# Attention passes: partial sums of a group handed to VectorE in two parts, by PSUM bank

## The chip, the cores and the metric

One core of one Trainium2 chip runs the whole program. The metric is the device time of one launch in microseconds (us). The kernel before takes 9238.56 us (median of 3 runs, 9234.02 to 9243.33).

## The reference, cut to what matters

Four graph layers over 6250 nodes and 106,250 edges (50,000 both ways and one loop per node), the edges sorted by destination. The two layers that the change touches are attention layers:

```python
# L1: 4 heads of 32
x_l = x @ W_l + b_l;  x_r = x @ W_r + b_r
e = einsum(leaky_relu(x_l[src] + x_r[dst]), att)            # a score per edge and head
alpha = softmax of e over the edges of one dst
out = segment_sum(alpha * x_l[src], dst)
# L2: 1 head of 128
h = x @ W;  e = leaky_relu((h @ att_src)[src] + (h @ att_dst)[dst])
alpha = softmax of e over the edges of one dst
out = segment_sum(alpha * h[src], dst)
```

Each is added to the nodes and normalised, then comes the next layer. All in float32.

## The kernel before, in words

The function `attend` runs twice: `attend1` for L1 (`two_sided`, table `xl_table`, rows of 136 values) and `attend2` for L2 (`h_table`, rows of 129 values). Between the two, and after the second, other stages run; a stage begins when the one before it has ended on all engines.

The edges lie in tiles of 128. A **group** is G = 7 tiles; there are R = 126 groups; a **chunk** is CG = 9 groups. Since the edges are sorted by destination, those of one tile fall on a window of at most 128 neighbouring nodes that begins at `base`. The result `acc` holds features on the partitions and nodes along the free axis, so that a tile's contribution is added to `acc[:, base : base + 128]`.

A step of the pass is one turn of the loop over g (142 of them, `last_step = R + LAG + 1`), with LAG = 15 and a ring of RING = 19 gathered groups:

- **GpSimd** (POOL) issues 7 indirect DMAs per group, the gathers of `rows` (L1494). It waits only for a free slot of the ring (`msg_ready`).
- **SyncE** (SP) loads one-hot rows, node windows and flags.
- **TensorE** (PE) does, in this order in step g: `expand(g)` (L1554, L1557: what the destination gives, into `ps_x`), transposes of the softmax of a chunk in the steps that have one, `sums(g - 15)` (L1566: for each of 7 tiles one float32 matmul of messages and one-hot matrix, two passes each, into `ps_sum`), `fill_d(g - 14)` (L1537, into `ps_d`), more transposes.
- **ScalarE** (ACT) makes the two one-hot matrices: `one_hot_t(g + 1)` (L1633, L1636) and, from `ps_d`, `one_hot(g - 14)` (L1643 Square, L1645 Relu). It also does the exponentials and copies `alpha` back (L1659).
- **VectorE** (DVE) does, in step g: `message(g - 15)` (L1708, rows times alpha), the additions of group g - 16 (L1727, seven dependent adds of 128x128 from `ps_sum` into `acc`), the evaluation of `ps_x` (L1682 three times in attend1, L1687 once in attend2), `score(g)` (L1695, L1698), and a part of a chunk's softmax in 6 of 9 steps. The additions are spread among the `mix_in` calls: in attend1 one, then around the three `mix_in` calls two by two; in attend2 two before `mix_in` and five after it.

At a chunk's start the first addition is preceded by a scaling of one column (L1722).

Semaphores order the sums and the additions. `sums(g)` waits for `hot_ready`, `msg_ready` and until every addition of group g - 1 is done (`added_before(g)`); then all 14 matmuls run and `summed` rises by 1. The additions of group g wait for `summed >= g + 1`. So `ps_sum` (128 x 8 x 128 float32, which is two PSUM banks of 4 tiles each, the second with 3 used) belongs either to PE or to DVE. `msg` and `hot` have two buffers each, freed by `summed`.

Of the kernel before, what the change touches and what calls it, by code (L numbers as in the profile page):

```python
# [23 lines left out]
G = 7  # L24
# [1405 lines left out]
def attend(nc, c, o, name, table, table_w, window, window_w, acc, heads, att):  # L1430
# [6 lines left out]
    C = table_w // heads if two_sided else D // heads  # L1437
    banks = [(0, 3), (3, 6), (6, G)] if two_sided else [(0, G)]
    nb = len(banks)
    last_step = R + LAG + 1  # L1440

    with stage(nc, name) as st:
# [3 lines left out]
        hot_t, hot = st.sb("hot_t", [P, 2, G, P]), st.sb("hot", [P, 2, G, P])  # L1446
        mix, red = st.sb("mix", [P, G, table_w]), st.sb("red", [P, G])
        msg = st.sb("msg", [P, 2, G, D])
# [9 lines left out]
        ps_d, ps_sum = st.ps("d", [P, 8, P]), st.ps("sum", [P, 8, P])  # L1458
# [21 lines left out]
        added_before = lambda g: 1 + g * G + (g + CG - 1) // CG  # L1480

        def chunk_at(g, k):
            n, left = divmod(g - k, CG)
            return n - 1 if left == 0 and 1 <= n <= NCH else None

        with nc.Block() as block:
            @block.gpsimd
            def _(pool):
                for g in range(R):
                    if g >= RING:  # L1490
                        pool.wait_ge(msg_ready, g - RING + 1)
                    for j in range(G):
                        t = g * G + j
                        pool.indirect_dma_start(  # L1494
                            rows[:, g % RING, j, :], None, table,
                            bass.IndirectOffsetOnAxis(ap=o.other[:, t:t + 1].bitcast(U32), axis=0)
                        ).then_inc(fetched[g % RING], 16)
# [33 lines left out]
            def _(pe):  # L1531
# [29 lines left out]
                def sums(g):  # L1561
                    pe.wait_ge(hot_ready, g + 1)
                    pe.wait_ge(msg_ready, g + 1)
                    pe.wait_ge(added, added_before(g))
                    for j in range(G):
                        mm = pe.matmul(ps_sum[:, j, :], msg[:, g % 2, j, :], hot[:, g % 2, j, :], start=True, stop=True)  # L1566
                    mm.then_inc(summed, 1)

                def turn_scores(n):
                    pe.wait_ge(scored, (n + 1) * CG)  # L1570
# [33 lines left out]
                for g in range(last_step):  # L1604
                    k0, k1, k2, k3, k4, k5 = (chunk_at(g, k) for k in range(6))
                    if g < R:
                        expand(g)
                    if k0 is not None:
                        turn_scores(k0)
                    if k1 is not None:  # L1610
                        turn_edges(k1, 0)
                    if k2 is not None:
                        turn_carries(k2, 0)
                    if 0 <= g - LAG < R:
                        sums(g - LAG)
                    if 0 <= g - LAG + 1 < R:
                        fill_d(g - LAG + 1)
                    if k3 is not None:
                        turn_edges(k3, 1)
                    if k4 is not None:  # L1620
                        turn_carries(k4, 1)
                        spread_factor()
                    if k5 is not None:
                        turn_alpha(k5)

            @block.scalar
            def _(act):
                def one_hot_t(g):
                    out = hot_t[:, g % 2]
                    act.wait_ge(rel_in[g % 2], 16 * (g // 2 + 1))  # L1630
                    if g >= 2:
                        act.wait_ge(expanded, nb * (g - 1))
                    act.activation(out, rel_all[:, g % 2, :].rearrange("p (j e) -> p j e", e=P), ACT.Square,  # L1633
                                   bias=c.minus_lane[:, 0:1]).then_inc(squared_t, 1)
                    act.wait_ge(squared_t, g + 1)
                    act.activation(out, out, ACT.Relu, bias=c.ones[:, 0:1], scale=-1.0).then_inc(hot_t_ready, 1)  # L1636

                def one_hot(g):
                    out = hot[:, g % 2]
                    act.wait_ge(filled, g + 1)  # L1640
                    if g >= 2:
                        act.wait_ge(summed, g - 1)
                    act.activation(out, ps_d[:, 0:G, :], ACT.Square).then_inc(squared, 1)  # L1643
                    act.wait_ge(squared, g + 1)
                    act.activation(out, out, ACT.Relu, bias=c.ones[:, 0:1], scale=-1.0).then_inc(hot_ready, 1)  # L1645

                def exponents(n):
                    act.wait_ge(carries_out, 2 * n + 1)
                    act.activation(fade[:], fade[:], ACT.Exp).then_inc(fade_ready, 1)
                    act.wait_ge(exp_in, n + 1)  # L1650
                    if n:
                        act.wait_ge(alpha_turned, n)
                    act.activation(p[:], mb[:], ACT.Exp).then_inc(exp_ready, 1)

                def alpha_back(n):
                    act.wait_ge(alpha_turned, n + 1)
                    if n >= 2:
                        act.wait_ge(msg_ready, (n - 1) * CG)
                    act.copy(alpha[:, n % 2], ps_alpha).then_inc(alpha_ready, 1)  # L1659

                one_hot_t(0)
                for g in range(last_step):
                    if chunk_at(g, 3) is not None:
                        exponents(chunk_at(g, 3))
                    if chunk_at(g, 6) is not None:
                        alpha_back(chunk_at(g, 6))
                    if g + 1 < R:
                        one_hot_t(g + 1)
                    if 0 <= g - LAG + 1 < R:
                        one_hot(g - LAG + 1)  # L1670

            @block.vector
            def _(dve):
# [26 lines left out]
                def message(g):  # L1700
                    n = g // CG
                    dve.wait_ge(alpha_ready, n + 1)
                    dve.wait_ge(fetched[g % RING], 16 * G * (g // RING + 1))
                    if g >= 2:
                        dve.wait_ge(summed, g - 1)
                    r = rows[:, g % RING, :, 0:heads * C].rearrange("p g (h d) -> p g h d", h=heads)[:, :, :, 0:D // heads]
                    w = of_group(alpha, g).rearrange("p g (h o) -> p g h o", o=1).to_broadcast([P, G, heads, D // heads])
                    dve.tensor_tensor(msg[:, g % 2].rearrange("p g (h d) -> p g h d", h=heads), r, w,  # L1708
                                      ALU.mult).then_inc(msg_ready, 1)

                def additions(g):
                    if not 0 <= g < R:
                        return
                    _, base = nc.values_load_multi_w_load_instructions(
                        o.base[0:1, g * 8:g * 8 + 8], engines=[dve.engine], min_val=0, max_val=N,
                        skip_runtime_bounds_check_because="keys are node numbers")
                    dve.wait_ge(summed, g + 1)
                    done = added_before(g)
                    if g % CG == 0:
                        dve.wait_ge(added, done)  # L1720
                        at = acc[:, bass.ds(base[0], 1)]
                        dve.tensor_scalar(at, at, factor[:, 0:1], None, ALU.mult).then_inc(added, 1)  # L1722
                        done += 1
                    for j in range(G):
                        dve.wait_ge(added, done + j)
                        at = acc[:, bass.ds(base[j], P)]
                        dve.tensor_tensor(at, at, ps_sum[:, j, :], ALU.add).then_inc(added, 1)  # L1727
                        yield
# [855 lines left out]
def gnn_kernel(nc, out, x_in, src, dst, length, edge_weight, real, p):  # L2584
    with ExitStack() as keep:
# [15 lines left out]
        with ExitStack() as first_layer:  # L2601
# [4 lines left out]
            with ExitStack() as sums:  # L2606
                scores = sums.enter_context(nc.sbuf_tensor("scores", [P, T * H0], F32))
                with ExitStack() as edges:
# [41 lines left out]
                      {"w": wo_t[:], "b": bo[:], "g": ln_g[:], "be": ln_b[:],  # L2650
                       "tables": (halves(0), halves(2), 2 * LW, [(xl_table, 0, LW), (xr_table, LW, LW)])}, by_dst)
        attend(nc, c, by_dst, "attend1", xl_table, LW, xr_table, LW, acc, H1,
               att_wide[:].rearrange("p h c -> p (h c)"))
        node_pass(nc, c, "update1", acc, x,
                  {"b": bias1[:], "tables": (h_wide[:], None, D + 2, [(h_table, 0, D + 1), (a_table, D + 1, 1)])})


        attend(nc, c, by_dst, "attend2", h_table, D + 1, a_table, 1, acc, 1, None)
        batch_norm_relu(nc, acc, {"bias": bias2[:, 0:1], "gamma": gamma[:], "beta": beta[:, 0:1]})
        x_table, conv_table = dram("x_table", [NP, D]), dram("conv_table", [NP, D])  # L2660
# [74 lines left out]
```

## Time and profile before

| | |
|---|---|
| median of 3 runs | 9238.56 us (9234.02 to 9243.33) |
| profiled execution, its own time | 9236.35 us |
| its span | 9234.6 us |
| busy share of the span | PE 60%, DVE 56%, ACT 25%, POOL 67% |
| attend1, first gather to last addition | 4159.4 to about 5426 us |
| attend2, first gather to last addition | 5501.4 to about 6770 us |
| mean granted TensorE clock | 0.663 of full speed |

The shares are means over all stages; the rows further down are read by stage. In the timeline rows the columns are the start in us, the duration in us, engine, line, operation, output<-inputs, shapes and count; in brackets stands how long the engine was idle before and what released it.

### The profile page before, as it was taken

The numbers are of one execution on the slowest core, as the hardware profiler recorded it, in microseconds if no ns is written. First come the engines' busy times: TensorE is split into PE (matmuls) and PEld (weight loads), VectorE is DVE, ScalarE is ACT, GpSimd is POOL, SyncE is SP. The second block draws the span as 40 slices with busy tenths as digits, with TensorE's granted clock in tenths as the row PEclk, the third lists the DMA queues.
The fourth block names the chain that finished last, engine by engine and source line by source line (L and its number), as shares of the span: only waits on it lengthen the run. The fifth ranks groups of instructions, "written<-read, shape, count | busy, mean of one in ns | idle before, by whom it ended". The sixth has DMA issues, their size and how long they took to land. (4 is left out here: it accounts for less than half of the span.)

```text
span 9234.6 us, 123780 instructions
## 1 busy us (share of the span) xinstructions
PE 5496.5 (60%) x32296; PEld 4870.9 (53%) x32296; DVE 5125.7 (56%) x14717; ACT 2272.5 (25%) x4142; POOL 6173.5 (67%) x6249
## 2 busy tenths in 40 slices
PE   6777757777729998036777755777733333333334
PEld 5666646777717776025666644666623333333333
DVE  7666654444479998045777743454554444444445
ACT  0111111111127776023444433444420000000000
POOL 2777755777717777757777717777627777577774
PEclk8555558888857777558899965555555555655556
DMA  1000006777716765015555533433311111211111
GB/s 30 2 2 2 2 23 188 210 209 210 208 37 161 166 162 129 2 55 141 137 138 135 131 33 77 78 78 78 64 32 53 52 52 53 55 52 52 52 53 47
DMA packets 877285, 793.86 MB, mean 86 GB/s; under 512 B 310468, under 2 KB 752200, under 8 KB 876542
## 3 DMA queue, kind: packets, MB, share of 16 engines
q1 hardware_dynamic: 535552, 375.25, 16.8%
q0 software_dynamic: 211680, 354.89, 15.7%
q10 hardware_dynamic: 129688, 59.67, 2.3%
q8 instruction: 130, 2.13, 0.1%
q14 instruction: 235, 1.93, 0.1%
HBM read 694.58 MB, written 94.60 MB: 85 GB/s over the span
## 5 line engine op out<-in xcount | busy, mean ns | idle before, releaser
L1426 PE MATMUL sum_ps_sum<-sum_hot,sum_msg 128*128 128x128 f32 x3528 | 842.0, 431 | 1413.3 <-DVE acc L1395 1361.7
L1426 PEld LDWEIGHTS sum_ps_sum<-sum_hot,sum_msg 128*128 128x128 f32 x3528 | 771.1, 330 | 1484.3 <-DVE acc L1395 1420.7
L558 POOL DMA_INDIRECT payload_dst<-place_dst_pay,place_dst_at_i x882 | 927.1, 1051 | 352.0 <-issue 303.7
L443 POOL DMA_INDIRECT payload_src<-load_src_pay_slot,load_src_at_i x882 | 862.4, 978 | 438.7 <-issue 275.8
L1370 POOL DMA_INDIRECT sum_rows<-x_table,dst_other x882 | 843.9, 957 | 457.7 <-issue 268.5
L1071 POOL DMA_INDIRECT scores_rows<-kv_table,scores_idx x882 | 834.0, 946 | 403.6 <-issue 250.5
L1494 POOL DMA_INDIRECT attend_rows<-h_table,dst_other x882 | 880.6, 998 | 306.1 <-issue 268.0
L1494 POOL DMA_INDIRECT attend_rows<-xl_table,dst_other x882 | 881.6, 1000 | 295.4 <-issue 268.5
L1370 POOL DMA_INDIRECT sum_rows<-conv_table,dst_other x882 | 843.9, 957 | 348.8 <-issue 268.5
L1566 PE MATMUL attend_ps_sum<-attend_hot,attend_msg 128*128 128x128 f32 x3528 | 677.2, 368 | 510.6 <-DVE acc L1727 510.6
L1566 PEld LDWEIGHTS attend_ps_sum<-attend_hot,attend_msg 128*128 128x128 f32 x3528 | 623.0, 273 | 555.2 <-issue 478.2
L1554 PE MATMUL attend_ps_x<-attend_win,attend_hot_t 128*128 128x136 f32 (+1 forms) x3528 | 759.4, 323 | 210.4 <-DMA attend_rows<-xl_table,dst_other 145.7
L1554 PEld LDWEIGHTS attend_ps_x<-attend_win,attend_hot_t 128*128 128x128 f32 x3528 | 657.5, 258 | 298.2 <-issue 256.2
L1727 DVE TENSOR_TENSOR acc<-acc,attend_ps_sum 128x128 f32 x1764 | 505.2, 286 | 274.6 <-PE attend_ps_sum L1566 125.9
L2128 ACT COPY conv_at<-acc 128x640 f32 (+1 forms) x20 | 14.5, 725 | 2282.0 <-PEq L2146 2266.4
L1643 ACT ACTIVATE attend_hot<-attend_ps_d 128x896 f32<-128x896 f32 x252 | 231.1, 917 | 1301.2 <-PE attend_ps_d L1537 1292.5
L369 PE MATMUL load_src_ps_look<-load_src_running,load_src_one_lo_t 128*128 128x50 f32 x1764 | 501.0, 399 | 0.0
L1383 DVE TENSOR_TENSOR sum_msg<-sum_rows,dst_weight 128x896 f32<-128x896 f32 x126 | 137.7, 1093 | 648.7 <-DMA sum_rows<-x_table,dst_other 648.7
L1383 DVE TENSOR_TENSOR sum_msg<-sum_rows,unit 128x896 f32<-128x896 f32 x126 | 137.6, 1092 | 647.2 <-DMA sum_rows<-conv_table,dst_other 647.2
L1105 PE MATMUL scores_ps_len<-const_ident,scores_length 128*128 128x128 f32 x1764 | 333.9, 365 | 248.6 <-ACT scores_hidden L1052 248.6
L369 PEld LDWEIGHTS load_src_ps_look<-load_src_running,load_src_one_lo_t 128*128 128x128 f32 x1764 | 453.9, 317 | 0.0
L1105 PEld LDWEIGHTS scores_ps_len<-const_ident,scores_length 128*128 128x128 f32 x1764 | 305.1, 267 | 266.7 <-issue 266.7
(441 smaller groups left out, 13655.0 us busy)
## 6 DMA issues: line engine op xcount, KB each, us to landing
attend_win<-xr_table SPq DMA_DIRECT2D x882, 68.0 KB
scores_win<-q_table ACTq DMA_DIRECT2D x882, 64.0 KB
spill<-scores_rows SPq DMA_DIRECT2D x126, 448.0 KB
place_dst_key_all<-key_rows_dst SPq DMA_DIRECT2D x126, 448.0 KB
place_dst_rows<-spill SPq DMA_DIRECT2D x126, 448.0 KB
attend_rel_all<-rel_flat_dst SPq DMA_DIRECT2D x252, 224.0 KB
place_dst_low_all<-low_rows_dst SPq DMA_DIRECT2D x126, 224.0 KB
payload_src<-load_src_pay_slot,load_src_at_i POOLq DMA_INDIRECT x882
```

Source lines behind the costliest of these rows:

```text
L369: pe.matmul(ps_look[:, j, 0:HB], one_lo_t[:, s, j, :], running[:, k, :], start=True, stop=True).then_inc(looked, 1)
L443: pool.indirect_dma_start(o.payload, bass.IndirectOffsetOnAxis(ap=at_i[:, s, j:j + 1].bitcast(U32), axis=0), pay_slot[:, s, j, :], None).t ...
L558: pool.indirect_dma_start(o.payload, bass.IndirectOffsetOnAxis(ap=at_i[:, t:t + 1].bitcast(U32), axis=0), pay[:, t, :], None).then_inc(sca ...
L1071: pool.indirect_dma_start(rows[:, s, j, :], None, table, bass.IndirectOffsetOnAxis(ap=idx[:, s, j:j + 1].bitcast(U32), axis=0)).then_inc(g ...
L1105: mm = pe.matmul(ps_len[:, j, :], length[:, s, j:j + 1].to_broadcast([P, P]), c.ident[:], start=True, stop=True)
L1370: pool.indirect_dma_start(rows[:, g % deep, j, :], None, table, bass.IndirectOffsetOnAxis(ap=o.other[:, t:t + 1].bitcast(U32), axis=0)).th ...
L1383: dve.tensor_tensor(msg[:, n], rows[:, s], over_tiles(group(alpha, g), D), ALU.mult).then_inc(msg_ready, 1)
L1426: mm = pe.matmul(ps_sum[:, n, j, :], msg[:, n, j, :], hot[:, n, j, :], start=True, stop=True)
L1494: pool.indirect_dma_start(rows[:, g % RING, j, :], None, table, bass.IndirectOffsetOnAxis(ap=o.other[:, t:t + 1].bitcast(U32), axis=0)).th ...
L1554: mm = pe.matmul(ps_x[:, bank, at:at + window_w], hot_t[:, g % 2, j, :], win[:, g % 3, j, :], start=True, stop=not two_sided)
L1566: mm = pe.matmul(ps_sum[:, j, :], msg[:, g % 2, j, :], hot[:, g % 2, j, :], start=True, stop=True)
L1727: dve.tensor_tensor(at, at, ps_sum[:, j, :], ALU.add).then_inc(added, 1)
```

## The change

`sums` waits, computes and signals twice per group: tiles 0 to 3 (first bank of `ps_sum`), then tiles 4 to 6 (second bank). Its first wait asks only that additions 0 to 3 of the group before are done, its second that all are. `summed` so rises by 2 per group, and the waits that free `hot` and `msg` count by two. In `additions` the wait for the sums moves behind the scaling of the column: addition 0 waits for the first half of the sums, addition 4 for the second.

```diff
+    halves = ((0, 4), (4, G))
...
                 def sums(g):
                     pe.wait_ge(hot_ready, g + 1)
                     pe.wait_ge(msg_ready, g + 1)
-                    pe.wait_ge(added, added_before(g))
-                    for j in range(G):
-                        mm = pe.matmul(ps_sum[:, j, :], msg[:, g % 2, j, :], hot[:, g % 2, j, :], start=True, stop=True)
-                    mm.then_inc(summed, 1)
+                    for j0, j1 in halves:
+                        pe.wait_ge(added, added_before(g) - (G - j1 if g else 0))
+                        for j in range(j0, j1):
+                            mm = pe.matmul(ps_sum[:, j, :], msg[:, g % 2, j, :], hot[:, g % 2, j, :], start=True, stop=True)
+                        mm.then_inc(summed, 1)
...
                     if g >= 2:
-                        act.wait_ge(summed, g - 1)
+                        act.wait_ge(summed, 2 * (g - 1))
...
                     if g >= 2:
-                        dve.wait_ge(summed, g - 1)
+                        dve.wait_ge(summed, 2 * (g - 1))
...
-                    dve.wait_ge(summed, g + 1)
                     done = added_before(g)
...
                     for j in range(G):
+                        if j == halves[0][0] or j == halves[1][0]:
+                            dve.wait_ge(summed, 2 * g + (1 if j == 0 else 2))
                         dve.wait_ge(added, done + j)
```

## Rows read from the trace of the kernel before

**Rows 1.** Page, costliest groups: gathers of attend2; busy, mean ns, idle before.
```profile
L1494 POOL DMA_INDIRECT attend_rows<-h_table,dst_other x882 | 880.6, 998 | 306.1 <-issue 268.0
```

**Rows 2.** Windows, instructions of attend_rows alone: PE, PEld, DVE, POOL busy, clock, DMA.
```profile
4159.40:4290.40 131.00, 49.33 (x196) 40.73 (x196) 0.00 (x0) 99.27 (x105) 0.77 0.59 148
4290.40:5309.50 1019.10, 344.35 (x1554) 275.11 (x1554) 119.59 (x110) 782.25 (x777) 0.91 0.54 135
5501.40:5632.40 131.00, 0.00 (x0) 0.00 (x0) 2.31 (x14) 99.27 (x105) 0.50 0.43 86
5632.40:6650.60 1018.20, 0.00 (x0) 0.00 (x0) 137.96 (x220) 781.30 (x777) 0.56 0.39 78
```

**Rows 3.** Waits, attend2 from 5632 us: us in total, times, longest.
```profile
POOL attend_rows L1494 <- DVE attend_msg L1708: 0.6, 2, 0.3
```

**Rows 4.** Timeline, attend2: a message and the gather that began inside it.
```profile
6258.37 1.09 DVE L1708 TENSOR_TENSOR attend_msg<-attend_rows,attend_alpha 128x896 f32<-128x896 f32 x1
6258.47 1.81 POOL L1494 DMA_INDIRECT attend_rows<-h_table,dst_other  x1 [0.30 <-issue]
```

**Rows 5.** Timeline, attend2: the last full cycle of PE and DVE, step 125.
```profile
6654.66 3.33 PE L1566 MATMUL attend_ps_sum<-attend_hot,attend_msg 128*128 128x128 f32 x14 [2.34 <-DVE acc L1727]
6657.92 0.92 PE L1537 MATMUL attend_ps_d<-const_minus_pick,attend_rel 8*128 8x512 bf16 x2
...
6658.77 3.15 PE L1554 MATMUL attend_ps_x<-attend_win,attend_hot_t 128*128 128x1 f32 x14
...
6662.01 0.17 DVE L1687 TENSOR_TENSOR attend_red<-attend_ps_x,attend_rows 128x7 f32<-128x7 f32 x1 [3.18 <-PE attend_ps_x L1554]
6662.15 1.97 DVE L1727 TENSOR_TENSOR acc<-acc,attend_ps_sum 128x128 f32 x5
...
6664.26 3.19 PE L1566 MATMUL attend_ps_sum<-attend_hot,attend_msg 128*128 128x128 f32 x14 [2.34 <-DVE acc L1727]
```

**Rows 6.** Timeline of POOL: the last gather of attend2.
```profile
6649.61 0.94 POOL L1494 DMA_INDIRECT attend_rows<-h_table,dst_other  x1 [0.30 <-issue]
```

**Rows 7.** Timeline, attend2, step 0: the group's last gather and its first reader.
```profile
5508.90 0.94 POOL L1494 DMA_INDIRECT attend_rows<-h_table,dst_other  x1 [0.30 <-issue]
...
5512.31 0.17 DVE L1687 TENSOR_TENSOR attend_red<-attend_ps_x,attend_rows 128x7 f32<-128x7 f32 x1 [4.33 <-DMA attend_rows<-h_table,dst_other]
```

**Rows 8.** Timeline, attend1: the last expand, and the sums behind it.
```profile
5313.18 0.47 PE L1554 MATMUL attend_ps_x<-attend_win,attend_hot_t 128*128 128x136 f32 x2 [2.02 <-DMA attend_rows<-xl_table,dst_other]
...
5318.00 1.80 PE L1566 MATMUL attend_ps_sum<-attend_hot,attend_msg 128*128 128x128 f32 x14 [1.34 <-DVE acc L1727]
```

**Rows 9.** Timeline, end of attend2: the last two groups.
```profile
6757.20 3.33 PE L1566 MATMUL attend_ps_sum<-attend_hot,attend_msg 128*128 128x128 f32 x14 [2.23 <-DVE acc L1727]
...
6760.66 2.81 DVE L1727 TENSOR_TENSOR acc<-acc,attend_ps_sum 128x128 f32 x7 [2.61 <-PE attend_ps_sum L1566]
...
6762.37 1.04 ACT L1645 ACTIVATE attend_hot<-attend_hot,const_ones 128x896 f32<-128x896 f32 x1
...
6763.61 3.33 PE L1566 MATMUL attend_ps_sum<-attend_hot,attend_msg 128*128 128x128 f32 x14 [2.23 <-DVE acc L1727]
6767.08 2.80 DVE L1727 TENSOR_TENSOR acc<-acc,attend_ps_sum 128x128 f32 x7 [3.61 <-PE attend_ps_sum L1566]
```

**Rows 10.** Timeline, attend2: the last chunk's alpha, the additions, the sums.
```profile
6708.90 1.09 DVE L1708 TENSOR_TENSOR attend_msg<-attend_rows,attend_alpha 128x896 f32<-128x896 f32 x1 [4.18 <-ACT attend_alpha L1659]
6709.91 2.79 DVE L1727 TENSOR_TENSOR acc<-acc,attend_ps_sum 128x128 f32 x7
...
6712.85 3.33 PE L1566 MATMUL attend_ps_sum<-attend_hot,attend_msg 128*128 128x128 f32 x14 [5.81 <-DVE acc L1727]
```

**Rows 11.** Windows, all instructions: PE, PEld, DVE, ACT, POOL busy, clock, DMA.
```profile
4400.00:5300.00 900.00, 657.84 (x4515) 581.10 (x4515) 695.00 (x1781) 394.06 (x425) 691.06 (x686) 0.91 0.54 136
...
5700.00:6600.00 900.00, 672.88 (x3067) 581.14 (x3068) 442.96 (x1482) 385.66 (x420) 690.98 (x686) 0.55 0.40 78
```

**Rows 12.** Timeline of DVE: the last additions of attend1.
```profile
5423.12 2.81 DVE L1727 TENSOR_TENSOR acc<-acc,attend_ps_sum 128x128 f32 x7 [3.61 <-PE attend_ps_sum L1566]
```

## The prediction, made before the kernel ran

> **What bounds the kernel now.** I read the page's list of costliest groups first. The reader is to see there that a pass's 882 gathers keep POOL busy for 880.6 us, with 306.1 us of idle time that is almost all "issue" [rows 1]. The waits then say that POOL lost 0.6 us to a full ring [rows 3]. So in both attention passes the gather stream is never held back by the consumers' semaphores, and the windows of the gathers measure it: attend1 from 4159.4 to 5309.5 us, attend2 from 5501.4 to 6650.6 us [rows 2]. What is left of a pass is its tail, from the last gather to the last addition: attend1's ends at 5423.12 + 2.81 = 5425.9 us, 116 us later [rows 12]; attend2's at 6767.08 + 2.80 = 6769.9 us, 119 us later [rows 9]. The change touches PE and DVE only, so it can win in these two tails and nowhere else, except that DVE can slow the gathers: one that began inside a message took 1.81 us instead of the 0.94 of others and ended 0.82 us after that message [rows 4, 6]. The first 105 gathers of a pass, before any message, took 1.248 us each, the other 777 1.312 us: 49.7 us in attend1 and 48.9 in attend2, which over some 110 messages is 0.45 us per message [rows 2].
>
> All of this is reckoned on the profiled execution, 9236.35 us (span 9234.6), which is 2.2 us below the median of the runs; that goes on top at the end.
>
> **The change part by part.**
>
> *What it adds.* One wait and one signal on PE and one wait on DVE per group, 126 groups and two passes. Queued behind PE's second wait are sums 4 to 6, fill_d and the next expand; behind DVE's the additions 4 to 6, score and the next message. No row shows such a wait alone. It costs nothing if what it waits for is done. The largest it can be is a bare hand-over: from the end of the last addition to the matmul, 6763.47 to 6763.61, 0.14 us [rows 9]; 252 times that is 35 us if all of them lay on the path. While gathers run they don't. On the path are at most the 32 tail steps: 0 to 4 us. I take 0, since the row nearest to it, the 2.81 us of seven additions in one row, has room for four additions (1.61 us) while the second half of the sums (3/7 of 3.33 = 1.43 us) runs [rows 9].
>
> *Steps during the gathers, attend2.* PE and DVE take turns here. Sums begin at 6654.66, fill_d 3.26 us later, expand 0.85 after that, the evaluation of it 3.24 later, five additions end after 0.14 + 1.97, and 0.14 later the next sums begin: 9.60 us [rows 5]. A group's gathers take 1018.2 / 111 = 9.17 us [rows 2]. So these steps are slower than the gathers, and the consumers fall behind; steps with a faster clock and the even mix of both kept it near. At the end they are late: the last gather's issue ended at 6650.55 and DVE evaluated that group at 6662.01, 11.5 us later [rows 5, 6], where 2.5 us are enough when nothing else is late (5509.84 to 5512.31) [rows 7]. With the change the sums start after additions 2 and 3 instead of 2 to 6: 0.70 us instead of 1.97, hence a cycle of 9.60 - 1.27 = 8.33 us, below 9.17. The heavy steps of the last chunk leave a lateness that three steps at 0.8 us each pay back for the most part. The most that can come of it is 11.5 - 2.5 = 9.0 us, the least nothing; I take 8.
>
> *Attend1 at the same place.* The last expand waited 2.02 us for its gather to land [rows 8]: nothing is late, so no gain. Its sums follow 1.34 us after the expand; half of them could fill that gap.
>
> *The tail's steady steps.* Before: sums 3.33, additions 2.81, hand-overs, 6.41 us from sums to sums [rows 9]. One would halve that. But a second chain runs beside it: fill_d (behind the sums on PE), Square, Relu, and only then the next sums, whose one-hot matrix this is. Relu ended at 6763.41 and the additions at 6763.47 [rows 9]. So with the additions out of the way the sums start some 0.06 to 0.1 us earlier and no more: **the one-hot chain is late next**. Where fill_d ran at the fast clock, in a good half of its 0.92 us, the gap is 0.3 to 0.5 us. Over the 9 steps behind the last alpha I read 1.6 us in attend2 and 1.7 in attend1. In the first six tail steps DVE also has the softmax parts, the additions end later, and the gap is larger: step by step, with the four additions in place of seven, 3.5 us in attend2 and 1.7 in attend1, where DVE itself sets most of these steps.
>
> *The last alpha.* The message waits for it, the additions for the message, the sums for the additions: 6709.91 to 6712.85 [rows 10]. Four additions take 1.61 instead of 2.79: 1.15 us in each pass.
>
> *The very last group.* The additions began after all sums and took 2.80 us [rows 9]. Now four lie beside the second half of the sums and three remain, 1.2 us: 1.6 us in each pass.
>
> *The waits of hot and msg, counted by two,* stand for the same event as before: 0. *The scaling of the column* can now run before the sums are there: 0.25 us in steps that the gathers cover: 0.
>
> *The gather stream.* The number of messages is the same; only when they fall against the gathers changes. No sign can be told beforehand. At best messages would cost the gathers nothing (-49 us per pass), at worst 0.87 each (0.42 more times 110, +46 per pass). By the nearest rows, both passes' windows, the offset was 0.45 and 0.44 in two passes with quite different steps [rows 2]; I take 0, and 0.1 us per message either way, 11 us per pass, as what may well happen.
>
> On what blocks what, the Trainium skill (SBUF — State Buffer, on the engine ports) says that VectorE with two SBUF inputs and GpSimd lock each other out of a shared port pair for a whole instruction. The rows agree for the message, and additions, which read PSUM and SBUF, leave gathers at 0.94 us. By that rule splitting the additions does nothing to the gathers; only moved messages do.
>
> *Sum.* Attend2: 8 + 3.5 + 1.15 + 1.6 + 1.6 = 15.9 us. Attend1: 1.7 + 1.15 + 1.7 + 1.6 = 6.2 us. Together 22 us: 9236.35 - 22 = 9214.3, and 2.2 for the median: **9217 us**, 0.24% less.
>
> **Rivals.** *A, only the tails gain.* Attend2's lateness stays, because heavy steps or SP's window loads refill it, and the extra waits take some back: -5 to -14 us, 9225 to 9234. For it: lateness had both signs over the pass. Against: a cycle 0.8 us below the gathers' pace.
>
> *B, slower: messages fall worse against the gathers.* Once DVE is no longer late it follows the gathers' landing, so that a message falls at nearly the same place of a gather in each step. If that is the bad place, the offset goes from 0.45 to 0.65 us: +0.2 x 221 = +44 us, less 22: 9260. It decides from 0.1 us more per message on, where it eats the whole gain. For it: the rows show 0.87 for one message [rows 4]. Against: the softmax parts spread the messages over many places. The same mechanism with the other sign gives 9195 or less.
>
> *C, slower: the clock falls in attend1.* PE is busy 73% there at a granted clock of 0.91 [rows 11]. The waits between PE's bursts move together into one longer gap before the next expand. Sums take 3.33 us at the slow level and 1.80 at the fast one [rows 8, 9]. At 0.91, about 18% of the time is slow; work at full clock is then 0.731 / 1.15 = 0.63 of the time, and all of it slow 1.17: +17% of 1019 us = +175 us at the most. It decides below a clock of about 0.66. Against it: a slower PE has shorter gaps, which raises the clock again.
>
> The Trainium skill (TensorE: Matmul & The Clock Gate, psum-queue depth-cycling) warns of just such bursts by bank, between which TensorE idles and its clock goes up and down. The trace has both levels already and no row with the new gaps; by that page of the skill the result would be C.
>
> **How the numbers follow.** This measurement can tell about 0.2%, 18 us, from no change. My forecast (9207 to 9226) 0.50, of which 0.38 beyond 18 us, the rest within; A 0.24, all within; B 0.10, of which 0.07 slower and 0.03 within; the better side of B 0.12, faster; C and costs that no row shows 0.04, of which 0.03 slower. Faster 0.50, same 0.40, slower 0.10. The range, 9194 to 9240 us, takes in A and 0.1 us per message either way in one pass or most of both.
>
> **What would show it.** Right: in attend2 the evaluation of the last group some 3 us after its last gather instead of 11.5; in tail steps the sums released by ACT's Relu, not by the additions, and steps of 6.3 us; last sums to last addition 1.6 us shorter. Wrong: gather windows that differ from 1019 us by over 15; tail steps well under 6 us (then the one-hot chain was not the next); a clock in attend1 under 0.85; a lateness of over 6 us still at attend2's end.

## The result, and the profile after

The changed kernel takes 9200.3 us (median of 5 runs, 9193.4 to 9208.4), the kernel before 9240.7 us on the same chip: ratio 0.9955, interval [0.9944, 0.9966]. It is faster by 0.45%, about twice the 0.24% forecast: inside the range, 17 us below the predicted 9217. The two profiled executions differ by 33.4 us where the medians differ by 40.4; what follows explains the 33.4.

The stages of the two profiled executions, each bounded by the first and last gather of a pass and its last addition (us, from the rows' times):

```
                              before    after     diff    forecast
up to attend1                 4159.4   4159.0     -0.3       0
attend1, gather stream        1150.1   1142.8     -7.3       0
attend1, tail                  116.5    111.2     -5.3      -6.2
between the passes              75.5     73.1     -2.4       0
attend2, gather stream        1149.2   1142.2     -7.0       0
attend2, tail                  119.3    102.5    -16.8     -15.9
after attend2                 2464.8   2470.3     +5.5       0
span                          9234.6   9201.2    -33.4     -22
```

The tails give what they were to give, 22.1 us for 22. A further 14.3 us come from the gather streams, where the forecast stood at nothing, with 11 us either way per pass. There is one profile of the kernel before; two of the changed kernel (the second is the experiment `change_again`) differ by 1.2 and 2.9 us in their streams. The stages outside the passes differ by a few us with both signs: in a second profile of the same changed kernel they read 4163.9, 75.2 and 2465.7 us.

The windows of the gathers, attend_rows alone, in the kernel after; columns as in [rows 2], which they answer. The first window of each pass holds the 105 gathers before any message, the second the other 777:

```profile
4159.03:4290.51 131.48, 49.88 (x196) 41.41 (x196) 0.00 (x0) 99.48 (x105) 0.74 0.58 147
4290.51:5301.84 1011.33, 364.45 (x1554) 296.48 (x1554) 119.82 (x110) 774.72 (x777) 0.88 0.54 136
...
5617.40:6628.40 1011.00, 0.00 (x0) 0.00 (x0) 139.82 (x222) 774.46 (x777) 0.57 0.40 79
```

The reader is to see that the first window is within 0.5 us of its length before, and that the second is 7.8 and 7.2 us shorter, and that this is POOL's own busy time (774.5 for 781.3 us in attend2). Gathers became shorter; none had waited.

Waits of DVE in attend2's gathers (us in all, times, longest), before and then after:

```profile
DVE attend_red L1687 <- PE attend_ps_x L1554: 239.1, 91, 3.7
DVE acc L1727 <- PE attend_ps_sum L1566: 77.9, 48, 2.5
...
DVE attend_red L1687 <- DMA attend_rows<-h_table,dst_other: 24.0, 7, 6.3
```
```profile
DVE attend_red L1689 <- DMA attend_rows<-h_table,dst_other: 344.3, 87, 6.9
DVE attend_msg L1710 <- ACT attend_alpha L1661: 32.1, 13, 2.8
DVE attend_red L1689 <- PE attend_ps_x L1555: 31.2, 13, 4.5
```

Before, DVE waited for PE in 91 steps and for the landing of the rows in 7; now it waits for the landing in 87. So attend2's consumers are no longer late. From a group's last gather to its evaluation it was 2.3 to 9.0 us (mean of a chunk) and 11.45 at the last group; it is 1.7 to 2.5 us, and 3.5 at the last. That place after, which answers [rows 5, 6]:

```profile
6627.45 0.94 POOL L1495 DMA_INDIRECT attend_rows<-h_table,dst_other  x1 [0.30 <-issue]
6631.92 0.17 DVE L1689 TENSOR_TENSOR attend_red<-attend_ps_x,attend_rows 128x7 f32<-128x7 f32 x1 [7.46 <-DMA attend_rows<-h_table,dst_other]
6632.05 0.71 DVE L1730 TENSOR_TENSOR acc<-acc,attend_ps_sum 128x128 f32 x2
...
6632.91 3.33 PE L1568 MATMUL attend_ps_sum<-attend_hot,attend_msg 128*128 128x128 f32 x14 [4.08 <-DVE acc L1730]
6632.96 1.13 DVE L1730 TENSOR_TENSOR acc<-acc,attend_ps_sum 128x128 f32 x3 [0.20 <-DVE acc L1730]
```

And the end of attend2, which answers [rows 9]:

```profile
6717.19 1.12 DVE L1730 TENSOR_TENSOR acc<-acc,attend_ps_sum 128x128 f32 x3 [0.20 <-DVE acc L1730]
...
6718.43 1.04 ACT L1647 ACTIVATE attend_hot<-attend_hot,const_ones 128x896 f32<-128x896 f32 x1
...
6719.53 3.36 PE L1568 MATMUL attend_ps_sum<-attend_hot,attend_msg 128*128 128x128 f32 x14 [2.08 <-ACT attend_hot L1647]
6721.74 1.55 DVE L1730 TENSOR_TENSOR acc<-acc,attend_ps_sum 128x128 f32 x4 [2.42 <-PE attend_ps_sum L1568]
6722.82 0.92 PE L1538 MATMUL attend_ps_d<-const_minus_pick,attend_rel 8*128 8x512 bf16 x2
...
6725.82 3.22 PE L1568 MATMUL attend_ps_sum<-attend_hot,attend_msg 128*128 128x128 f32 x14 [2.08 <-ACT attend_hot L1647]
6728.03 1.55 DVE L1730 TENSOR_TENSOR acc<-acc,attend_ps_sum 128x128 f32 x4 [3.42 <-PE attend_ps_sum L1568]
6729.78 1.13 DVE L1730 TENSOR_TENSOR acc<-acc,attend_ps_sum 128x128 f32 x3 [0.20 <-DVE acc L1730]
```

Three things are to be seen. The sums wait for ACT's Relu (6718.43 + 1.04, sums at 6719.53) while the additions had ended at 6718.31, 1.2 us earlier. Sums follow sums after 6.29 us, where it was 6.41. And at the very end the additions finish 5.09 us after the sums began, where it was 6.27.

### The profile page after: what moved, and what is told of

It reads as the page before. It is cut to its first block and busy times, and to the rows that moved or that the text cites. A ratio compares the mean times of both kernels' runs of the same rounds, so it can differ in the third digit from the quotient of the medians.

```text
span 9201.2 us, 124032 instructions
## 1 busy us (share of the span) xinstructions
PE 5531.8 (60%) x32296; PEld 4904.6 (53%) x32296; DVE 5119.4 (56%) x14717; ACT 2274.6 (25%) x4142; POOL 6169.1 (67%) x6249
```

## The experiments

The first eight runs fell to chips on which the kernel before takes 11,598 us (four runs) and 11,603 us (the three repeats and the long delay): their profiles show gathers held by full buffers for some 420 to 610 us in each pass. The releasers in the profile point at SyncE's loads rather than at the gathers. In attend2 of the first of these kernels PE waited 123.8 us for node windows to land and ACT 294.7 us for another load; on the chip of the result, in the kernel before, it was 26.7 us and nothing. Why these chips differ stays open. Their gather streams are therefore not compared with the chip of the result. The last four ran on a chip where the kernel before takes 9241 us.

A tail begins at the last gather, so it contains how late the consumers are at that moment, and on the slow chips that is 25 to 40 us. What can be compared on all chips is the part from the evaluation of the last group to the last addition (us, from the rows' times; the mean step is from the sums of group 117 to those of 125):

```
                                  attend1   attend2   mean step in each
before                              111.0     107.9     6.37  6.35
after                               104.2      99.0     6.03  6.03
after, second profile               104.2     100.1     6.03  6.04
split in the last groups alone      105.2      99.0     6.16  6.04
split everywhere else alone         110.7     108.0     6.31  6.32
  the same, other slow chip         110.6     108.3     6.30  6.32
split, 0.3 us of delay in attend2   104.1      99.5     6.03  6.03
  the same, other slow chip         104.2      99.3     6.04  6.03
split, 0.9 us of delay in attend2   104.2     105.2     6.04  6.16
split and fill_d first               86.7      78.2     3.93  3.88
  the same, other slow chip          86.6      78.2     3.93  3.88
fill_d first, no split              110.6     106.4     6.38  6.37
```

Between kernels whose tails are alike, but for the longer delay, it agrees within 1.2 us, whatever the chip.

**The split in the last groups alone.** Only groups from 110 on are split:

```
+    parts = lambda g: halves if g >= 110 else ((0, G),)
...
-                    for j0, j1 in halves:
+                    for j0, j1 in parts(g):
```

> The split in two halves only for groups 110 to 125, whose sums run after the last expand; before that as in the kernel before. Theory (tail steps win by themselves, lateness needs the split during the gathers): gathers of attend1 and attend2 last 1150 and 1149 us as before, tail of attend1 111 us instead of 116.5, tail of attend2 some 111 instead of 119.3, the last group of attend2 still evaluated some 11 us after its last gather; in all -13 us against before. Rival (the whole gain comes from the steps during the gathers): no difference beyond noise, within 3 us in both tails.

Measured: ratio 0.9989 [0.9973, 1.0005], so no difference in the whole that is clear of noise; tails 132.2 and 138.9 us, steady steps 6.29 us. From the last evaluation on it takes 5.8 and 8.9 us less than the kernel before, nearly all that the whole change wins there (6.8 and 8.9).

**The split everywhere else alone.** The same with `g < 110`.

> The split only for groups 0 to 109, so in every step that has gathers; the tail steps as in the kernel before. Theory: attend2's last group evaluated some 2 to 3 us after its last gather, its tail 119.3 - 9 = 110 us, attend1's 116 us; the gathers of each pass again some 7 us shorter than before (1143 and 1142 us) because the messages follow the gathers at fixed places; in all -23 us. Rival (the 14 us of the gathers are chance from run to run): gathers at 1150 and 1149 us, in all -9 us.

Measured: ratio 0.9967 [0.9952, 0.9982]; tails 143.5 and 142.8 us, steady steps 6.41 us. The kernel with the whole change and a short delay in attend2 (below) has 129.4 and 134.3 us on this chip. Of these 14.1 us in attend1, 7.5 are lateness at the last evaluation (32.7 us for 25.2), whose origin was not sought; the tail code gives the other 6.6, and all of the 8.5 in attend2. What the split gives in the stream can't be read here, where full buffers hold the gathers whatever the consumers do.

The same on another such chip:

> The split only for groups 0 to 109, tail steps as in the kernel before, once more: the first time the chip's transfers were so slow that the gathers waited for the ring (the kernel before took 11598 us there). If the gathers are not held by the ring here: theory, as said for the first run: attend2's last group evaluated 2 to 3 us after its last gather, tail 110 us instead of 119.3, gathers 1143 and 1142 us, in all -23 us. Rival (the gathers' 14 us are chance): 1150 and 1149 us, in all -9.

0.9975 [0.9961, 0.9989], tails 143.4 and 143.2 us.

**Fill_d ahead of the sums, with the split.** This tests the claim that the one-hot chain (fill_d, Square, Relu) is next in the tail:

```
-                    if 0 <= g - LAG < R:
-                        sums(g - LAG)
                     if 0 <= g - LAG + 1 < R:
                         fill_d(g - LAG + 1)
+                    if 0 <= g - LAG < R:
+                        sums(g - LAG)
```

> The changed kernel with one more edit: fill_d of the next group stands before the sums of this one on PE, so that the one-hot matrix of the next group is made while these sums run. Theory (in the changed kernel the one-hot chain behind the sums ends last in tail steps): they go from 6.29 us to about 4.6 (PE needs 3.33 + 0.92 = 4.25 at the slow clock, DVE 1.09 + 2.81 = 3.90), 12 or 13 such steps a pass, each tail some 20 us shorter, in all about -42 us against the changed kernel. Rival (the additions or the hand-overs between PE and DVE bound the step): steps of over 6 us still, within 5 us of the changed kernel.

Measured: ratio 0.9923 [0.9906, 0.9940]; tails 119.0 and 110.1 us. PE, DVE and ACT in attend2's tail, timeline:

```profile
8641.09 1.04 ACT L1647 ACTIVATE attend_hot<-attend_hot,const_ones 128x896 f32<-128x896 f32 x1
...
8641.24 2.17 PE L1568 MATMUL attend_ps_sum<-attend_hot,attend_msg 128*128 128x128 f32 x14 [1.14 <-DVE acc L1730]
8641.29 1.13 DVE L1730 TENSOR_TENSOR acc<-acc,attend_ps_sum 128x128 f32 x3 [0.20 <-DVE acc L1730]
8642.34 1.08 DVE L1710 TENSOR_TENSOR attend_msg<-attend_rows,attend_alpha 128x896 f32<-128x896 f32 x1
8643.34 1.54 DVE L1730 TENSOR_TENSOR acc<-acc,attend_ps_sum 128x128 f32 x4
...
8644.88 1.04 ACT L1647 ACTIVATE attend_hot<-attend_hot,const_ones 128x896 f32<-128x896 f32 x1
8645.03 2.43 PE L1568 MATMUL attend_ps_sum<-attend_hot,attend_msg 128*128 128x128 f32 x14 [1.14 <-DVE acc L1730]
```

A step is 3.79 us: three additions, message, four additions, and a hand-over of 0.15. DVE alone sets it, with PE waiting 1.14 us for `acc` in each; the Relu that the sums of 8645.03 need had ended at 8642.13, and the one at 8644.88 serves the next group. PE runs partly at the fast level here (2.17 and 2.43 us for 14 matmuls that take 3.33 at the slow one); other steps, such as the next but one, take 4.1 us. The forecast's "late next" holds. Against the kernel with the split and a short delay it is 43 us faster on this chip, where 42 were expected, and 63 on the other; each ratio is uncertain by some 20 us.

> The changed kernel with fill_d of the next group before the sums of this one, once more. On the slow chip its tails were 119 and 110 us, those of the others 129 to 143. Theory (one-hot chain late in the changed kernel's tail): here tails of some 91 and 83 us instead of 111 and 102.5, in all -40 us against the changed kernel. Rival: tail steps of 6 us, within 5 us of the changed kernel.

0.9925 [0.9908, 0.9942], tails 121.8 and 108.8 us: the same.

**Fill_d ahead of the sums, without the split** (the same move in the kernel before):

> The kernel before, with fill_d issued on PE ahead of the sums; no split by bank. Theory 'two chains end within 0.1 us of each other': sums and additions alone need 3.33 + 0.14 + 2.81 + 0.14 = 6.42 us a step, so without the split the tail steps stay at 6.3 to 6.42 us, although the one-hot chain is 2 to 3 us early; no gain in the tails beyond 2 us each. Rival 'the one-hot chain alone is what counted': tail steps of 3.8 to 4.6 us as in the kernel with both, and tails some 20 us shorter each.

Measured: 9215.5 us, ratio 0.9972 [0.9962, 0.9983]. End of attend2's tail:

```profile
6731.66 0.92 ACT L1643 ACTIVATE attend_hot<-attend_ps_d 128x896 f32<-128x896 f32 x1 [4.31 <-PE attend_ps_d L1537]
6732.61 1.04 ACT L1645 ACTIVATE attend_hot<-attend_hot,const_ones 128x896 f32<-128x896 f32 x1
...
6733.85 3.33 PE L1566 MATMUL attend_ps_sum<-attend_hot,attend_msg 128*128 128x128 f32 x14 [2.23 <-DVE acc L1727]
6737.32 2.81 DVE L1727 TENSOR_TENSOR acc<-acc,attend_ps_sum 128x128 f32 x7 [2.61 <-PE attend_ps_sum L1566]
6740.27 3.33 PE L1566 MATMUL attend_ps_sum<-attend_hot,attend_msg 128*128 128x128 f32 x14 [3.09 <-DVE acc L1727]
```

The Relu that ends at 6733.65 made the matrix of the last sums, which begin at 6740.27: it is 6.6 us early, and still they wait for seven additions, 6.42 us a step. So in steady steps either edit alone gives 0 to 0.12 us and both together 2.6; in the mean over the last eight steps, where PE's clock varies, the split alone gives 0.3 us, fill_d first nothing, both 2.4 to 2.5. Attend1's tail is 116.1 us, as expected. Attend2's is 110.0, 9.4 us less than before, where at most 2 were expected: 7.9 of it is lateness, 3.5 us at the last group for 11.45. By the terms of [rows 5], fill_d out of the gap between sums and expand takes 0.85 us from the 9.60 us cycle, and that too brings it under the gathers' 9.17.

**Where the stream's 14 us come from.** What the 882 gathers of a pass take beyond 0.944 us each was 49.0 and 48.0 us, and is 41.6 and 41.1. Counted over attend2's rows, a message costs the gathers nothing, or at most 0.05 us, where it begins in the first 0.33 us of a gather's 1.25 us; from there it costs its place less 0.29 us, up to 0.9, and nothing in the last 0.03. The first idea was that messages fall at fixed places once DVE follows the landings, so that a delay ahead of the message moves them. A memset on an idle buffer of DVE does it, attend2 only: 0.30 us in one kernel, three of 0.31 in the other.

```
+                    if not two_sided:
+                        dve.memset(mix[:].rearrange("p j w -> p (j w)")[:, 0:288], 0.0)
```

> The changed kernel with a memset of 288 columns of an unused scratch tile on DVE just before each message of attend2, some 0.3 us. Theory (in attend2 the message stands at a fixed place of the gather that it meets, and costs the gathers by that place alone): moving every place of the changed kernel's trace by 0.3 us takes the cost from 39.6 to 17 us, so the gathers of attend2 last 1120 us instead of 1142; attend1 as in the changed kernel; in all -22 us although DVE has 38 us more work. Rival (places are random, the cost is a mean of 0.4 us per message wherever it stands): gathers unchanged within 4 us, in all 0 to +3 us.

> 0.3 us of memset on DVE before each message of attend2, once more. Where DVE follows the gathers' landing and the ring never holds POOL: theory of fixed places: attend2's gathers 1120 us instead of 1142, in all -22 us against the changed kernel; rival of random places: 1142 us, in all 0 to +3.

> The changed kernel with three memsets of 300 columns before each message of attend2, some 0.85 us. Theory of fixed places: moving the places of the changed kernel's trace by 0.8 to 0.9 us takes the cost of the messages from 39.6 to between 45 and 51 us: gathers of attend2 1148 to 1153 us, some 30 us longer than with 0.3 us of memset, and +6 to +11 against the changed kernel. Rival of random places: as with 0.3 us, 1142 us.

Measured: 0.9972 [0.9957, 0.9987], 0.9977 [0.9960, 0.9993] and, with 0.92 us, 0.9961 [0.9948, 0.9975]. The excess of attend2's gathers over 0.944 us was 19.4 and 15.1 us with the short delay and 35.9 with the long. In the five runs without a delay on these chips it was 6.8 to 22.5, so the short delay shows nothing; the long one lies above all others. The gathers also stood 417 to 464 us before full buffers there, so the totals say nothing either. Inconclusive for the 14 us.

**The message made small.** DVE multiplies one tile of seven; the edit is the same in both kernels:

```
-    dve.tensor_tensor(msg[:, g % 2].rearrange(...), r, w,
+    dve.tensor_tensor(msg[:, g % 2].rearrange(...)[:, 0:1], r[:, 0:1], w[:, 0:1],
```

> Left out: the message of six of the seven tiles of a group (its buffer is zeroed at the start and the sums read it as before), so the message takes about 0.2 us instead of 1.09. Its pair is the changed kernel with the same left out. Theory 'the gathers pay for messages': what the 882 gathers of a pass take beyond 0.944 us each, 49 and 48 us in the kernel before, falls below 12 us a pass, as a gather can be held only while a message runs. Rival 'the excess comes from the transfers or from other work of DVE': it stays above 30 us.

> The changed kernel with the same left out: the message of six of seven tiles. Theory 'what the change won in the streams it won at the messages': the streams of this kernel and of its pair without the split are equal within 3 us a pass, and it is faster than its pair by the tails alone, 17 to 24 us. Rival 'the streams are shorter for another reason': it is 33 to 40 us faster than its pair, and the streams differ by 6 to 8 us a pass as in the full kernels.

Measured: 9186.1 us without the split, 0.9940 [0.9927, 0.9954], and 9128.7 with it, 0.9876 [0.9861, 0.9891]. Spans of the stages:

```
                              without    with     diff
attend1, gather stream        1106.3    1107.0    +0.6
attend1, tail                  115.5     108.8    -6.7
attend2, gather stream        1117.4    1104.1   -13.3
attend2, tail                  140.3     104.3   -36.1
```

The excess over 0.944 us falls to 5.2 and 1.6 us without the split, 5.8 and 3.0 with it. So the gathers' excess is the messages' doing, and with it gone attend1's streams are alike: what the change won there, it won at the messages. In attend2 the expectation failed: the pair differs by 49 us in this pass, since the kernel without the split falls behind. Waits of POOL in its attend2, and two evaluations at the end:

```profile
POOL attend_rows L1494 <- DVE attend_msg L1708: 16.9, 7, 5.0
```
```profile
6573.41 0.95 POOL L1494 DMA_INDIRECT attend_rows<-h_table,dst_other  x1 [0.30 <-issue]
...
6597.60 0.17 DVE L1687 TENSOR_TENSOR attend_red<-attend_ps_x,attend_rows 128x7 f32<-128x7 f32 x1 [2.93 <-PE attend_ps_x L1554]
...
6607.20 0.17 DVE L1687 TENSOR_TENSOR attend_red<-attend_ps_x,attend_rows 128x7 f32<-128x7 f32 x1 [3.18 <-PE attend_ps_x L1554]
```

The evaluations are 9.60 us apart, the cycle of [rows 5], while seven unhindered gathers take 8.74. Lateness grew to 32.8 us, until the buffers were full. It is the messages' toll on the gathers that had kept the kernel before from this.

That gives the mechanism of attend2. A gather that a message holds ends 0.82 us after that message, and the next ones are counted from there. So after a held gather the next message's place follows from the interval S between the two messages alone: S - 1.09 - 0.82 - 0.30, less whole cycles of 1.248. For S = 9.60 this is 7.39 - 5 x 1.248 = 1.15. Two messages of the kernel before, with the gathers they hold:

```profile
6319.93 1.08 DVE L1708 TENSOR_TENSOR attend_msg<-attend_rows,attend_alpha 128x896 f32<-128x896 f32 x1
6320.03 1.80 POOL L1494 DMA_INDIRECT attend_rows<-h_table,dst_other  x1 [0.30 <-issue]
6322.14 0.95 POOL L1494 DMA_INDIRECT attend_rows<-h_table,dst_other  x1 [0.30 <-issue]
...
6329.53 1.08 DVE L1708 TENSOR_TENSOR attend_msg<-attend_rows,attend_alpha 128x896 f32<-128x896 f32 x1
6329.62 1.82 POOL L1494 DMA_INDIRECT attend_rows<-h_table,dst_other  x1 [0.30 <-issue]
```

Both begin at 1.15 us of the cycle, just before the next gather, nearly the dearest place: 0.86 us. Of attend2's 18 intervals of 9.5 to 9.7 us before, 16 end there; and behind a message that cost over 0.05 us the formula gives the next place within 0.06 us in 73 of 80. A late consumer with a cycle of 9.60 locks itself to that place, which slows seven gathers to its own pace (8.74 + 0.86 = 9.60). These 16 messages cost 13.7 us, the other 94 only 0.35 us each; at 0.35 the 16 would cost 8 us less, and attend2's stream became 7.0 us shorter. With the change, DVE follows the landing, and places repeat from chunk to chunk. The message of the ninth group, as here, costs nothing in 11 of 12 chunks, that of the seventh in all 12, and that of the fourth 0.7 to 0.9 us in all 12:

```profile
6025.27 1.14 DVE L1710 TENSOR_TENSOR attend_msg<-attend_rows,attend_alpha 128x896 f32<-128x896 f32 x1
6025.29 0.94 POOL L1495 DMA_INDIRECT attend_rows<-h_table,dst_other  x1 [0.30 <-issue]
```

Messages that cost at most 0.05 us are 47 of 111 for 30 of 110, those that cost over 0.7 us 41 for 40; the mean is 0.36 us for 0.42, and 0.33 in the second profile. Messages spread evenly over the cycle would cost 0.35, by the rule above. So in sum the change's places are no better than an even spread; what it ended is the lock. That the lock is worth these 7 us is reckoned from one profile of the kernel before, and borne out by `fill_first_before`, whose attend2 isn't late either: 0.32 us per message.

**The change once more**, beside these on one chip:

> The changed kernel itself, beside the three others, so that one chip has the change and the kernels that take it apart. Theory 'tails and places': on a chip where the gathers land in time, -35 to -42 us against the kernel before (tails -22, gather streams -14). On a chip where landings hold the gathers for hundreds of us the streams say nothing, and only the tails are left: attend1's 129 to 130 us and attend2's 134 us, as in the two kernels with the change and an added delay, where the kernel with the split for gathers alone had 143.4 and 143.2. Rival 'the split adds a wait that costs': tail steps above 6.41 us.

9197.8 us, 43 less than the kernel before where 35 to 42 were expected, ratio 0.9949 [0.9936, 0.9963]; tails 111.1 and 104.0 us, excess 42.8 and 38.1. Both streams are shorter again, by 6.1 and 9.9 us. The kernel with fill_d first and no split has 44.8 and 36.5: where attend2 isn't late, its stream is short, by whichever edit. Its attend1 stream too is 4.1 us shorter than before.

The best version seen is the split with fill_d ahead of the sums: 78 and 90 us below the kernel before on its chips. It was not run on a chip of the result's kind; there the two parts of it gave 43 and 25 us one by one.

## Why the prediction came out as it did

*What bounds the kernel.* Right. The gather stream was never held, and the tails were the only place of a sure gain.

*Attend2's lateness and first tail steps, 8 + 3.5 = 11.5 us.* Measured 11.9: from the last gather to the sums of group 110 it was 13.7 us and is 4.5 (-9.2, of which 7.9 lateness); the six steps behind it gave 2.7. The cycle of 9.60 us was read right; the pair with small messages shows it bare.

*Attend1's first part, 1.7 us.* Measured 0. The first steps gave 0.2 us, and the last expand took it back. It now waited longer for its rows and then ran at the slow level at first:

```profile
5305.64 0.79 PE L1555 MATMUL attend_ps_x<-attend_win,attend_hot_t 128*128 128x136 f32 x2 [3.10 <-DMA attend_rows<-xl_table,dst_other]
...
5310.51 1.05 PE L1568 MATMUL attend_ps_sum<-attend_hot,attend_msg 128*128 128x128 f32 x8
```

It takes 4.9 us up to the sums, where it was 4.8 with their wait of 1.34 us [rows 8]: half of the sums did fill that gap, and the slow matmuls (0.66 us for 0.40) ate it.

*The last alpha, 1.15 us a pass.* Measured 1.25 and 1.23 (10.44 to 9.19 and 10.29 to 9.06 us).

*The steps behind it, 1.7 and 1.6 us.* Measured 2.8 and 2.55. The steady step is 6.29 us, as forecast. The first two behind the alpha gave more, 0.7 and 0.9 us each in attend2: 5.92 and 5.53; in the second the sums ran partly at the fast level (2.60 us for 3.33).

*The very last group, 1.6 us a pass.* Measured 1.2. From the start of the sums it was to take 3.33 + 0.14 + 1.2 = 4.67 us and takes 5.09: the four additions begin 2.21 us after the sums and take 1.55, so they end 0.54 us after the last sum (6729.58 and 6729.04), and the last three begin 0.20 later. The term let the last three follow the sums; they follow the first four, whose 1.6 us don't fit beside the 1.43 of the second half.

*The waits added.* Nothing on the path of a steady step, as taken. The prediction also said that such a wait costs nothing if what it waits for is done. Here the fifth addition begins 0.20 us after the fourth, where without a wait it is 0.13 (6768.62 to 6768.75 in the kernel before). The difference of 0.07 us lies in the shadow of the one-hot chain but for the last group.

*The gather stream, 0 with 11 us either way per pass.* Here the term was off: -7.3 and -7.0 us, inside what was named and not chosen. The step that failed is "By the nearest rows, both passes' windows, the offset was 0.45 and 0.44 in two passes with quite different steps; I take 0": a term put at nothing. In attend2 the 0.44 was no draw of chance but held the lock at 1.15 us: by direct count its messages cost 0.42 us in the mean, and 0.35 without those 16. The rows to see it were there, 16 intervals of one length with messages at one place, and the mean of a window hid them. For attend1 the runs show that its 7 us lie at the messages, not why they fall better now: by direct count a message there cost 0.41 us, and 0.33 and 0.36 in the two profiles after. That stays open.

The prediction also took the shared port as a lock of both sides against each other. The rows show one side: a gather that begins inside a message is held, but the 68 messages of attend2 that began inside a running gather took 1.08 to 1.09 us, no longer than others. Nothing of the sum hangs on it.

*Rivals.* A (9225 to 9234) didn't come: the lateness stayed away. B was right that places repeat once DVE follows the landings, but in sum they cost what an even spread costs, so the change of 0.06 to 0.09 us per message has its better sign and, in attend2, comes from the end of the lock. C came in a small measure. PE's granted clock in attend1's gathers fell from 0.91 [rows 11] to 0.88, 0.87 in the second profile, and 0.93 to 0.88 in the pair with small messages, and PE was 37 us longer busy over 900 us:

```profile
4400.00:5300.00 900.00, 694.38 (x4541) 615.84 (x4542) 696.54 (x1786) 395.84 (x428) 689.62 (x691) 0.88 0.54 136
```

The gathers covered it all but at the last expand. The Trainium skill (TensorE: Matmul & The Clock Gate, psum-queue depth-cycling) warns of bursts by bank with idle time between; the trace agrees in direction, and over the whole span the mean clock was 0.661 for 0.663.

## What to carry to other kernels

Where two engines take turns over one group, hand it over in parts, and then look at the chain that ended 0.06 us before: in this tail splitting alone gave 0.12 us in a steady step, moving a small operation of the other chain alone nothing, and the two together up to 2.6 of 6.4. When a stage is bounded by a stream of DMA issues that another engine's operation can hold, don't take the mean toll as given: list at which point of the stream's cycle each such operation begins, for a consumer that is late can lock itself to the dearest point. A faster consumer then shortens a stream that it never held by a semaphore.

## What the runs showed of the hardware

- A 1.09 us message of DVE holds the gather issue that begins inside it: the issue ends 0.82 us after the message, which costs 0 to 0.9 us, and at most 0.05 if the message begins in the first 0.33 us of the gather's 1.25 us cycle. A gather issue under way is not held (0.94 to 0.95 us in attend2 before), and doesn't hold the message. With a message of one tile of seven the toll of a pass fell from 41 to 49 us to 1.6 to 5.8.
- One program took 9241 us on two chips and 11,598 to 11,603 on two others: in the profile of the kernel with the split in its tail alone, from one of these, POOL waited for free buffers 1034.7 us in the two passes.

```profile
POOL attend_rows L1496 <- DVE attend_msg L1711: 1034.7, 138, 94.5
```
